# Fetching 33 of 1,568 gathered chunks row by row from SyncE and ScalarE in a two-layer graph kernel

## The chip, the cores and the metric

The kernel runs on one core of one Trainium2 chip. The metric is the device time in microseconds (us) of one execution. PE is TensorE (matmuls), DVE is VectorE, ACT is ScalarE, POOL is GpSimd, SP is SyncE, which here only issues DMAs.

## What is computed

A graph with 6,250 nodes of 128 features and 100,000 edges, sorted by receiver (`dst`), passes two message layers with a residual and a layer norm after each. Cut to what matters here:

```python
# layer 0
h = features @ W_lin.T
ef = shifted_softplus(basis(edge_weight) @ Wf1 + bf1) @ Wf2 + bf2
messages = h[senders] * ef                       # one row of h for each edge
agg = segment_sum(messages, receivers)
x = layernorm(x + shifted_softplus(agg @ Wm1 + bm1) @ Wm2 + bm2)
# layer 1
h = silu(emb @ mlp_w0 + b0); h = silu(h @ mlp_w1 + b1); w = h @ mlp_w2 + b2
ss, vv = xs[senders], xv[senders]                # one row of the new table for each edge
m = products of w, ss, vv and the unit vector of the edge
out = segment_sum(m, receivers) through W_out0, W_out1
x = layernorm(x + out / 16)
```

Both layers read one row of 128 floats (512 bytes) of a table for every edge, by the edge's sender. That read is the gather that the change is about.

## The kernel before

The edges are padded to 196 halves of 512 edges. A half has 4 chunks of 128 edges, and a pair is two halves. Each layer walks over the 196 halves. Everything is written out as straight code; every engine has its own program, and semaphores order them.

The table of a layer (`h_table` in layer 0, `up_table` in layer 1) lies in HBM. POOL gathers it: for each chunk it issues one indirect DMA (L479) that reads 128 rows by the numbers in `senders` and writes them into one of 4 slots of `sent`, a slot holding a half. Before the gathers of half n it waits until the half n-4 has been used (semaphore `msg`). So POOL issues 784 gathers in each layer.

In layer 0, SP loads the distances of a pair into `basis` (L556, L559) and stores a part of them back to HBM once ACT has worked on them (L566, `radial_embedding`). ACT makes the basis of a pair (L679, L682). PE multiplies it (`hidden0`, L885), DVE caps the sum (L1207), ACT takes exponential and logarithm (L689, L691), DVE finishes the softplus (L1216), PE applies the second weight (`filter0`, L833 and the bias L835), and DVE multiplies filter and gathered rows into `msg` (`msg0`, L1226). DVE makes the one-hot matrix of the receivers (L1187), PE sums the messages with it into a window (`window_sums`, L848), and DVE adds the window (L1200).

In layer 1, SP loads the embedding of a pair (L581, `emb_in`). PE and ACT run a small network on it (PE L904, ACT L735, PE L912, ACT L742, then `filter1`, PE L833). DVE builds `msg` in six steps (`msg1`, from L1242, which is the first to read the gathered rows, to L1261, which releases the slot), and PE sums two windows (L848, 16 matmuls a half). When the sums of 512 receivers are complete, PE runs an output unit between two halves (L1018).

The engines are staggered: at step h of its loop PE does `hidden` for half h, `filter` for half h-3 and `window_sums` for half h-5, and DVE does `msg` for half h-4. In layer 0, ACT does at step h the exponential and the logarithm of half h-2, and at every even step the basis of the pair that begins at h.

Between the layers POOL waits until all of `up_table` is stored.

## Time and profile before

| what | value |
|---|---|
| median of 3 timed runs | 2057.03 us (2056.96 to 2058.91) |
| the profiled execution, its own time | 2045.77 us |
| its span, first to last instruction | 2044.0 us |
| POOL busy | 1496.7 us, 73% |
| PE busy | 1784.7 us, 87% |
| DVE busy | 1409.2 us, 69% |
| ACT busy | 635.8 us, 31% |
| granted PE clock, mean | 0.872 of full speed |

The profiled execution is 11.3 us shorter than the median of the timed ones. Layer 0 fills the stretch from about 40 to 1,020 us of the span, and layer 1 that from about 1,040 to 2,035 us. Time in which an engine sits between two of its own instructions without waiting for another is called "issue" in the profile; on POOL it is the pause after each gather.

### The profile page before, as it was taken

Reading aid. Unit: us, or ns where it says so; the run is one execution under the profiler, and the core shown is the slowest. Engines: PE = TensorE matmul, PEld = TensorE weight load, DVE = VectorE, ACT = ScalarE, POOL = GpSimd, SP = SyncE. Lnnn points to the kernel's source line nnn. Section 1 sums busy time; section 2 is a strip of 40 time slices with the busy share of each in tenths; the row PEclk is TensorE's granted clock in tenths of the full one; section 3 lists DMA queues with packets and bytes.
Section 4 is the critical chain, followed back from the end, with each engine's and each line's share of the span. In section 5 each row is a group of like instructions: output and inputs, shape, how many; then the busy total and the mean of one; then the engine's idle time right before and its main releaser. Section 6 shows DMA issues by size and latency. Waiting matters only on the chain.

```text
span 2044.0 us, 30183 instructions
## 1 busy us (share of the span) xinstructions
PE 1784.7 (87%) x10130; PEld 1340.0 (66%) x10130; DVE 1409.2 (69%) x3184; ACT 635.8 (31%) x951; POOL 1496.7 (73%) x1610
## 2 busy tenths in 40 slices
PE   4877777877888778787869999999999999999997
PEld 4655665655666556565637777777766777777776
DVE  4785555656566666666647687687777777777876
ACT  4554443444444444444241111121121111112211
POOL 5777777777777777777647777777777777777774
PEclk8878778888788898889869898899899899889989
DMA  7322222222222232222311222222222222222232
GB/s 207 100 81 80 83 77 83 81 79 80 80 80 80 80 84 80 81 79 81 108 46 53 56 58 57 57 57 57 57 58 57 57 57 57 57 57 57 57 102 53
DMA packets 99487, 150.69 MB, mean 74 GB/s; under 512 B 33916, under 2 KB 59174, under 8 KB 99230
## 3 DMA queue, kind: packets, MB, share of 16 engines
q0 software_dynamic: 50656, 103.11, 18.7%
q1 hardware_dynamic: 48336, 43.56, 7.0%
q10 hardware_dynamic: 336, 2.01, 0.3%
q8 instruction: 87, 1.43, 0.3%
q14 instruction: 72, 0.59, 0.1%
HBM read 135.33 MB, written 13.21 MB: 73 GB/s over the span
## 4 chain that ended last, share of the span: by engine, by line
POOL 44%; PE 33%; issue 15%; DVE 2%; DMA 2%; ACT 1%; SPq 1%; DVEq 0%; POOLq 0%; ACTq 0%
POOL sent L479 44%; PE bank L848 15%; PE bank L833 7%; PE bank L912 3%; PE bank L904 3%; PE bank L835 2%; PE bank L1018 1%; PE bank L932 1%; DMA sent<-up_table,senders 1%; DMA radial_embedding<-basis 0%; ACT unit_in L650 0%; DMA x_sb<-in_x 0%; ACT unit_in L648 0%; DMA basis<-near_lengths 0%; PE bank L795 0%
## 5 line engine op out<-in xcount | busy, mean ns | idle before, releaser
L479 POOL DMA_INDIRECT sent<-up_table,senders x784 | 739.8, 944 | 267.7 <-issue 234.4
L479 POOL DMA_INDIRECT sent<-h_table,senders x784 | 739.9, 944 | 258.7 <-issue 237.8
L848 PE MATMUL bank<-onehot,msg 128*128 128x128 f32 x4704 | 732.7, 314 | 4.2 <-DVE msg L1261 3.2
L848 PEld LDWEIGHTS bank<-onehot,msg 128*128 128x128 f32 x4704 | 651.1, 219 | 116.2 <-issue 104.0
L833 PE MATMUL bank<-Wf_sb,hid 128*128 128x128 f32 x1568 | 258.6, 316 | 179.7 <-DVE msg L1226 178.0
L833 PEld LDWEIGHTS bank<-Wf_sb,hid 128*128 128x128 f32 x1568 | 227.1, 223 | 205.2 <-DVE msg L1226 201.8
L1226 DVE TENSOR_TENSOR msg<-bank,sent 128x512 f32<-128x512 f32 x196 | 135.4, 691 | 310.7 <-issue 251.2
L833 PEld LDWEIGHTS bank<-w_sb,h 64*128 64x128 f32 x1568 | 191.4, 189 | 170.6 <-issue 127.3
L1187 DVE TENSOR_TENSOR onehot<-relT,bank 128x512 f32<-128x512 f32 x392 | 265.9, 678 | 8.8 <-PE bank L848 6.2
L689 ACT ACTIVATE soft<-soft 128x512 f32<-128x512 f32 x196 | 122.9, 627 | 444.5 <-DVE soft L1207 444.4
L1200 DVE TENSOR_TENSOR sums<-sums,bank 128x128 f32 (+1 forms) x392 | 136.6, 348 | 165.7 <-PE bank L848 161.4
L833 PE MATMUL bank<-w_sb,h 64*128 64x128 f32 x1568 | 229.2, 287 | 11.0 <-DVE msg L1261 10.8
L742 ACT ACTIVATE h<-bank,cols 128x512 f32<-128x512 f32 x98 | 67.3, 687 | 426.2 <-PE bank L912 426.2
L735 ACT ACTIVATE h<-bank,cols 128x512 f32<-128x512 f32 x98 | 67.3, 687 | 370.3 <-PE bank L904 370.3
L835 PE MATMUL bank<-bias,ones_bf 3*128 3x512 bf16 x405 | 166.3, 411 | 0.0
L1242 DVE TENSOR_TENSOR dots<-sent,bank 128x384 f32<-128x384 f32 x196 | 108.5, 554 | 76.7 <-DMA sent<-up_table,senders 71.8
L885 PE MATMUL bank<-basis,Wf_sb 50*128 50x256 f32 x784 | 146.9, 507 | 13.9 <-ACT basis L682 13.9
L1207 DVE TENSOR_SCALAR soft<-bank,cols 128x512 f32<-128x512 f32 x196 | 145.0, 740 | 13.7 <-PE bank L885 8.6
L1216 DVE SCALAR_TENSOR_TENSOR hid<-bank,cols,soft 128x512 f32<-128x512 f32 x196 | 145.8, 744 | 9.8 <-ACT soft L691 9.8
L691 ACT ACTIVATE soft<-soft,half_const 128x512 f32<-128x512 f32 x196 | 141.4, 721 | 6.4
L885 PEld LDWEIGHTS bank<-basis,Wf_sb 50*128 50x128 f32 x784 | 86.0, 236 | 63.3 <-issue 39.1
L912 PE MATMUL bank<-h,w_sb 128*128 128x512 f32 x196 | 117.6, 685 | 9.4 <-ACT h L735 9.4
(140 smaller groups left out, 1399.9 us busy)
## 6 DMA issues: line engine op xcount, KB each, us to landing
basis<-in_edge_weight SPq DMA_DIRECT2D x196, 100.0 KB
sent<-h_table,senders POOLq DMA_INDIRECT x784
sent<-up_table,senders POOLq DMA_INDIRECT x784
basis<-near_lengths SPq DMA_DIRECT2D x196, 16.0 KB
radial_embedding<-basis SPq DMA_DIRECT2D x196, 16.0 KB
emb_in<-radial_embedding SPq DMA_DIRECT2D x98, 32.0 KB
x_sb<-in_x SPq DMA_DIRECT2D x12, 256.0 KB, 7.2
h_table<-h SPq DMA_DIRECT2D x12, 256.0 KB, 4.2
```

The costliest lines, as they stand in the source:

```text
L479: pool.indirect_dma_start(sent[:, n % SLOTS, j, :], None, table, bass.IndirectOffsetOnAxis(pick, 0))\
L691: a.activation(tile_, tile_, ACT.Ln, scale=0.5, bias=half_const[:, :])\
L833: t_.matmul(out_bank[0:rows, j, :], lhs(j), weight, start=(j == 0), stop=False, skip_group_check=True)
L835: return t_.matmul(out_bank[0:rows, 0:n_tiles, :], ones_bf[:, 0:rows], bias3[:, which:which + 1, :].broadcast_to([3, n_tiles, P]), start=F ...
L848: last = t_.matmul(ps[:, k, :], msg[:, p, j, k * P:(k + 1) * P], onehot[:, p, j, :], start=(j == 0), stop=(j == HALF_CHUNKS - 1))
L885: last = t_.matmul(filtA[q.slot][:, cs], Wf1_sb[rows, :], basis[rows, q.pair_slot, cs], start=True, stop=True, skip_group_check=True)
L912: t_.matmul(bank[1][:, :], w1_sb[:], h1[:, g, :], start=True, stop=True)\
L1187: v.tensor_tensor(onehot[:, p], by_chunk(relT, h).rearrange("p (j a) -> p j a", a=1) .broadcast_to([P, HALF_CHUNKS, WINDOW]), numbers[p].r ...
L1200: v.tensor_tensor(here, here, ps[:, 0:outputs, :], ALU.add).then_inc(sm["added"], 1)
L1207: v.tensor_scalar(soft[:, p, :], filtA[h.slot][:, :], bf1_c, EXP_CAP, ALU.add, ALU.min)\
L1216: v.scalar_tensor_tensor(out=hid[:, p, :], in0=filtA[h.slot][:, :], scalar=bf1_s, in1=soft[:, p, :], op0=ALU.add, op1=ALU.max)\
L1226: v.tensor_tensor(msg[:, p, :, 0:P], filtB[0], sent[:, h.slot], ALU.mult)\
```

## The change

33 chunks, 13 in layer 0 and 20 in layer 1, are no longer gathered by POOL. SP and ACT fetch them instead, one DMA of 512 bytes for each row, 128 rows a chunk, into a buffer of their own (`by_rows_sp`, `by_rows_act`, two chunks deep). ACT then copies the finished chunk into its place in `sent`. The table `row_halves` says which engine takes which chunk of a half, from which half on, how many halves lie between two such chunks, and how many rows are fetched in one pair of halves:

| layer | engine | halves between chunks | rows in a pair | chunks |
|---|---|---|---|---|
| 0 | SP | 22 | 12 | 8 |
| 0 | ACT | 32 | 8 | 5 |
| 1 | SP | 16 | 16 | 11 |
| 1 | ACT | 20 | 13 | 9 |

The row numbers are read from `src_i` in SBUF into registers, at most 7 at a time (TENSOR_LOAD); each row then takes one register instruction (ISA) and one DMA. SP does this after its own DMAs of a pair, ACT after the work of each half, half of the pair's rows at a time. DVE waits for 48 instead of 64 on `landed` for a half with one such chunk, and for the copy (`s_placed`). To make room for new semaphores, two units of `x` share one load semaphore `d_x`. A few things change in the branch for unsorted receivers too, which this input does not take.

```diff
+class Rows:
+    def __init__(self, layer, engine, chunk, start, apart, rows, halves):
...
+        self.first = start + apart + 2
+        self.count = (halves - 2 - self.first) // apart + 1
...
+    row_halves = [Rows(0, "sp", 3, 8, 22, 12, halves),
+                  Rows(0, "act", 2, 8, 32, 8, halves),
+                  Rows(1, "sp", 3, 8, 16, 16, halves),
+                  Rows(1, "act", 2, 8, 20, 13, halves)]
...
+    by_rows = {e: sb(f"by_rows_{e}", [P, 2, P]) for e in sorted({r.engine for r in row_halves})}
...
-    d_x, d_bases, d_up = sems("d_x", len(units)), sem("d_bases"), sem("d_up")
+    d_x, d_bases, d_up = sems("d_x", -(-len(units) // 2)), sem("d_bases"), sem("d_up")
...
+    def fetch_rows(eng, engine_type, r, table, some, k):
+        if len(some) == 0:
+            return
+        if some[0] == 0:
+            wait(eng, s_placed[r], k - 1)
+        pair, column = r.place(k)
+        for first in range(some[0], some[-1] + 1, 7):
+            now = range(first, min(first + 7, some[-1] + 1))
+            _, numbers_now = nc.values_load_multi_w_load_instructions(
+                src_i[pair:pair + 1, column + now[0]:column + now[-1] + 1],
...
+            for i, number in zip(now, numbers_now):
+                eng.dma_start(by_rows[r.engine][i:i + 1, k % 2, :], table[bass.ds(number, 1), :])\
+                    .then_inc(d_by_rows[r][k % 2], 16)
...
-        def gather(sm, table):
+        def gather(sm, table, layer):
...
                 for j in range(HALF_CHUNKS):
+                    if j in chunks_by_rows(layer, n):
+                        continue
...
         def move_basis(h):
...
+            if h.real():
+                own_rows(0, h.rel, h_dram)
...
         for n in range(SLOTS, halves):
             load_embedding(Half(n, halves))
+            if n % 2 == 0:
+                own_rows(1, n, v_dram)
...
+        def place_rows(layer, sm, n):
+            for r in rows_of_layer(layer):
...
+                wait(act, d_by_rows[r][k % 2], (k // 2 + 1) * P * 16)
+                wait(act, sm["msg"], n - SLOTS + 1)
+                a.activation(sent[:, n % SLOTS, r.chunk, :], by_rows[r.engine][:, k % 2, :],
+                             ACT.Copy).then_inc(s_placed[r], 1)
...
         def layer0(h):
+            place_rows(0, L0, h.rel - 2)
...
+            own_rows(0, h, h_dram)
...
         def layer1(h):
+            place_rows(1, L1, h.rel - 2)
...
+            own_rows(1, h, v_dram)
...
-            wait(dve, L0["landed"][h.slot], h.uses(64))
+            rows_there(0, L0, h)
...
-            pe.wait_ge(d_x[u.rel], 16)
+            pe.wait_ge(d_x[u.rel // 2], 16 * min(2, len(units) - u.rel // 2 * 2))
```

Where this moves instructions: on POOL, in half 32 of layer 0, the first with a chunk of SP's, the gathers of four halves stood as follows before (one that carries the wait for the slot, and three more).

```order
L479 DMA sent<-h_table,senders 128x128 [waits L0_msg]
L479 DMA sent<-h_table,senders 128x128 x3
L479 DMA sent<-h_table,senders 128x128 [waits L0_msg]
L479 DMA sent<-h_table,senders 128x128 x3
L479 DMA sent<-h_table,senders 128x128 [waits L0_msg]
L479 DMA sent<-h_table,senders 128x128 x3
```

In the changed kernel the same place has three gathers in one half.

```order
L546 DMA sent<-h_table,senders 128x128 [waits L0_msg]
L546 DMA sent<-h_table,senders 128x128 x3
L546 DMA sent<-h_table,senders 128x128 [waits L0_msg]
L546 DMA sent<-h_table,senders 128x128 x2
L546 DMA sent<-h_table,senders 128x128 [waits L0_msg]
L546 DMA sent<-h_table,senders 128x128 x3
```

One gather is gone, and nothing stands in its place on POOL.

On SP in layer 1, the loads of the embedding followed one another with only the wait for PE's first matmul (`L1_filt1`) between them.

```order
L581 DMA emb_in<-radial_embedding 16x512 [waits d_emb1,d_emb0]
L581 DMA emb_in<-radial_embedding 16x512
L589 DMA up_table<-sums 128x4x128 [waits s_rows] x12
L589 DMA up_table<-sums 106x128 [waits s_rows]
L581 DMA emb_in<-radial_embedding 16x512 [waits L1_filt1] x96
```

In the changed kernel (L664 is that load) 16 rows stand behind each one while chunks are fetched: three loads of row numbers (7, 7 and 2) and 16 times a register instruction with a DMA. The end of one such block, the next load of the embedding, and the beginning of the next block:

```order
L448 TENSOR_LOAD src_i
L452 ISA
L452 DMA by_rows_sp<-up_table 1x128
L452 ISA
L452 DMA by_rows_sp<-up_table 1x128
L664 DMA emb_in<-radial_embedding 16x512 [waits L1_filt1]
L448 TENSOR_LOAD src_i
L452 ISA
L452 DMA by_rows_sp<-up_table 1x128
```

The next load of the embedding now comes after 35 instructions that were not there.

On ACT in layer 0, logarithm (L691), basis (L679, L682) and the next exponential (L689) followed each other.

```order
L689 ACTIVATE soft<-soft 128x512 [waits L0_capped]
L691 ACTIVATE soft<-soft,half_const 128x512 [waits L0_exped]
L679 ACTIVATE basis<-basis,neg_centers 122x512 [waits L0_r_in1]
L682 ACTIVATE basis<-basis,exp_bias,exp_scale 122x512 [waits L0_squared]
L689 ACTIVATE soft<-soft 128x512 [waits L0_capped]
L691 ACTIVATE soft<-soft,half_const 128x512 [waits L0_exped]
```

In the changed kernel (L774 and L776 are the exponential and logarithm, L764 and L767 the basis) four rows stand between a logarithm and what follows it.

```order
L776 ACTIVATE soft<-soft,half_const 128x512 [waits L0_exped]
L448 TENSOR_LOAD src_i
L452 ISA
L452 DMA by_rows_act<-h_table 1x128
L452 ISA
L452 DMA by_rows_act<-h_table 1x128
L452 ISA
L452 DMA by_rows_act<-h_table 1x128
L452 ISA
L452 DMA by_rows_act<-h_table 1x128
L764 ACTIVATE basis<-basis,neg_centers 122x512 [waits L0_r_in1]
```

So the basis, or the next exponential, can begin only when these nine instructions have been issued.

## Rows read from the trace of the kernel before

**Rows 1.** POOL's waits: engine line <- waited for: us in total, times, longest

```profile
POOL sent L479 <- issue: 472.2, 1549, 0.3
POOL sent L479 <- DVE msg L1261: 9.4, 14, 4.5
```

**Rows 2.** Timeline of POOL: start, us, engine, line; first and last gather of each layer

```profile
38.46 1.04 POOL L479 DMA_INDIRECT sent<-h_table,senders  x1 [19.84 <-DMA h_table<-h]
...
1016.29 0.94 POOL L479 DMA_INDIRECT sent<-h_table,senders  x1 [0.30 <-issue]
...
1041.12 0.94 POOL L479 DMA_INDIRECT sent<-up_table,senders  x1 [23.89 <-DMA up_table<-sums]
...
2023.75 0.94 POOL L479 DMA_INDIRECT sent<-up_table,senders  x1 [0.30 <-issue]
```

**Rows 3.** Page, costliest groups: line, operation, count, busy and mean ns, idle before

```profile
L1226 DVE TENSOR_TENSOR msg<-bank,sent 128x512 f32<-128x512 f32 x196 | 135.4, 691 | 310.7 <-issue 251.2
```

**Rows 4.** Windows of layer 1: busy us of each engine, PE clock, DMA share, GB/s

```profile
1090.00:1350.00 260.00, 260.00 (x1457) 194.08 (x1456) 195.17 (x486) 37.10 (x54) 196.60 (x209) 0.89 0.21 57
1350.00:1590.00 240.00, 230.66 (x1360) 170.28 (x1360) 179.18 (x470) 42.87 (x61) 181.48 (x193) 0.95 0.21 57
1590.00:1950.00 360.00, 360.00 (x2058) 268.03 (x2056) 274.94 (x722) 67.88 (x96) 272.00 (x289) 0.91 0.21 57
```

**Rows 5.** The same windows for line L1261 alone, one instruction a half

```profile
1090.00:1350.00 260.00, 15.24 (x54) 0.89 0.21 57
1350.00:1590.00 240.00, 13.53 (x48) 0.95 0.21 57
1590.00:1950.00 360.00, 20.38 (x72) 0.91 0.21 57
```

**Rows 6.** Timeline of PE in layer 1: window sums of two halves one pair apart

```profile
1150.80 3.52 PE L848 MATMUL bank<-onehot,msg 128*128 128x128 f32 x16
...
1161.12 3.58 PE L848 MATMUL bank<-onehot,msg 128*128 128x128 f32 x16
...
1220.69 2.05 PE L848 MATMUL bank<-onehot,msg 128*128 128x128 f32 x16
...
1229.37 0.82 PE L848 MATMUL bank<-onehot,msg 128*128 128x128 f32 x5
```

**Rows 7.** Chain that ended last, layer 1: start, us, what; one output unit

```profile
1635.68 1.91 PE bank L1018 x16
```

**Rows 8.** Timeline of SP and ACT in layer 0, and ACT's DMA at 45 us

```profile
45.11 0.81 ACT L682 ACTIVATE basis<-basis,exp_bias,exp_scale 122x512 f32<-122x512 f32 x1
45.12 0.32 ACTq L702 DMA_DIRECT2D sums<-in_edge_attr  x1
...
503.32 0.30 SPq L559 DMA_DIRECT2D basis<-near_lengths  x1
503.67 0.29 SPq L556 DMA_DIRECT2D basis<-in_edge_weight  x1
```

**Rows 9.** Timeline around the start of layer 1, PE, ACT and DVE

```profile
1039.55 2.06 PE L904 MATMUL bank<-emb_in,w_sb 16*128 16x512 f32 x2 [2.76 <-issue]
...
1047.92 0.25 ACT L669 ACTIVATE inverse_all<-inverse_all 128x52 f32<-128x52 f32 x1
...
1049.53 0.69 DVE L1187 TENSOR_TENSOR onehot<-relT,bank 128x512 f32<-128x512 f32 x1 [1.81 <-issue]
```

**Rows 10.** Timeline of ACT in layer 0, one pair, and the DVE step behind

```profile
503.09 0.72 ACT L691 ACTIVATE soft<-soft,half_const 128x512 f32<-128x512 f32 x1
...
506.92 0.63 ACT L689 ACTIVATE soft<-soft 128x512 f32<-128x512 f32 x1 [1.65 <-DVE soft L1207]
507.58 0.72 ACT L691 ACTIVATE soft<-soft,half_const 128x512 f32<-128x512 f32 x1
...
510.36 0.74 DVE L1216 SCALAR_TENSOR_TENSOR hid<-bank,cols,soft 128x512 f32<-128x512 f32 x1
```

**Rows 11.** Timeline of PE, first units of the table of layer 0

```profile
7.44 1.94 PE L787 MATMUL bank<-ident,x_sb 128*128 128x128 f32 x8 [1.74 <-DMA x_sb<-in_x]
```

More of the change, by code:

```diff
@@ L16 @@
 from contextlib import ExitStack
+import itertools
 import math
@@ L192, in each_unit, with number, iterations, place @@
     for_units(eng, nodes, own, 0)
+class Rows:
+    def __init__(self, layer, engine, chunk, start, apart, rows, halves):
+        self.layer, self.engine, self.chunk = layer, engine, chunk
+        self.start, self.apart, self.rows = start, apart, rows
+        self.first = start + apart + 2
+        self.count = (halves - 2 - self.first) // apart + 1
+        assert apart % 2 == 0 and apart // 2 * rows >= P
+    def number(self, n):
+        k, rest = divmod(n - self.first, self.apart)
+        return k if rest == 0 and 0 <= k < self.count else None
+    def iterations(self):
+        return [(self.first + k * self.apart) // SLOTS for k in range(self.count)]
+    def place(self, k):
+        n = self.first + k * self.apart
+        return n // 2, n % 2 * HALF + self.chunk * P
+    def of_pair(self, n):
+        k, rest = divmod(n - self.start, self.apart)
+        if not 0 <= k < self.count:
+            return None, range(0)
+        return k, range(min(rest // 2 * self.rows, P), min((rest // 2 + 1) * self.rows, P))
 def complete_after(edges, nodes, halves):
@@ L378, in build @@
     L0, L1 = edge_sems(0), edge_sems(1)
+    d_by_rows = {r: sems(f"d_by_rows_{r.engine}{r.layer}_", 2) for r in row_halves}
+    s_placed = {r: sem(f"s_placed_{r.engine}{r.layer}") for r in row_halves}
     every = [{k: sems(f"every{n}_{k}", 2) for k in ("onehot", "window", "added")} for n in range(2)]
@@ L524, in _, with own_rows @@
         wt_halves = edge_weight.rearrange("(n e) -> n e", e=HALF)
+        def own_rows(layer, n, table):
+            for r in rows_of_layer(layer):
+                if r.engine == "sp":
+                    k, some = r.of_pair(n)
+                    if n == r.start:
+                        sp.wait_ge(d_rows[0], 16)
+                        if layer == 0:
+                            for s in range(WIDE):
+                                sp.wait_ge(table0["stored"][s], stores_of(s))
+                        else:
+                            sp.wait_ge(s_table, 16 * len(units))
+                    fetch_rows(sp, mybir.EngineType.SP, r, table, some, k)
         def load_layer1_weights():
@@ L692, in soft_log, with own_rows @@
                 .then_inc(sm[n[1]], 1)
+        def place_rows(layer, sm, n):
+            for r in rows_of_layer(layer):
+                k = r.number(n)
+                if k is None:
+                    continue
+                wait(act, d_by_rows[r][k % 2], (k // 2 + 1) * P * 16)
+                wait(act, sm["msg"], n - SLOTS + 1)
+                a.activation(sent[:, n % SLOTS, r.chunk, :], by_rows[r.engine][:, k % 2, :],
+                             ACT.Copy).then_inc(s_placed[r], 1)
+        def own_rows(layer, h, table):
+            for r in rows_of_layer(layer):
+                if r.engine == "act" and h.real():
+                    k, rows = r.of_pair(h.rel - h.parity)
+                    if h.rel == r.start:
+                        act.wait_ge(d_rows[0], 16)
+                        if layer == 0:
+                            for s in range(WIDE):
+                                act.wait_ge(table0["stored"][s], stores_of(s))
+                        else:
+                            act.wait_ge(s_table, 16 * len(units))
+                    half = len(rows) // 2
+                    fetch_rows(act, mybir.EngineType.Activation, r, table,
+                               rows[half:] if h.parity else rows[:half], k)
         def layer0(h):
+            place_rows(0, L0, h.rel - 2)
             if h.parity == 0 and h.real():
@@ L1218, in soft0, with rows_there @@
                 .then_inc(L0["soft"], 1)
+        def rows_there(layer, sm, h):
+            last = h.counter.start * SLOTS + h.rel
+            fewer = sum(len(chunks_by_rows(layer, n)) for n in range(h.slot, last + 1, SLOTS))
+            wait(dve, sm["landed"][h.slot],
+                 h.counter.value(64, (h.rel // SLOTS + 1) * 64 - 16 * fewer))
+            for r in rows_of_layer(layer):
+                if h.counter.eng is None and r.number(h.rel) is not None:
+                    wait(dve, s_placed[r], r.number(h.rel) + 1)
         def msg0(h):
@@ L1240, in msg1 @@
             wait(dve, L1["ways"], h.upto())
-            wait(dve, L1["landed"][h.slot], h.uses(64))
+            rows_there(1, L1, h)
             v.tensor_tensor(dots[:, p], vec, dirs, ALU.mult).then_inc(L1["dots"], 1)
```

25 lines of the change are left out of this document (16 added, 9 removed).

## The prediction

> **What bounds the kernel now.** I read POOL's waits first [rows 1]. Of 1,568 gathers, 1,549 wait for nothing but their own pause of 0.3 us, and only 14 of layer 1 wait for DVE, 9.4 us in all. So POOL issues gathers without a break. Its timeline gives the price of one [rows 2]: in layer 0 (1016.29 - 38.46) / 783 = 1.249 us, in layer 1 (2023.75 - 1041.12) / 783 = 1.255 us, or 1.243 us without those 9.4 us. A half costs POOL 4.99 us.
>
> An engine that never rests need not be what the others wait for, so I read the consumers next, a layer at a time. In layer 0, DVE stands idle before `msg` L1226 for 310.7 us [rows 3], 1.59 us in each of 196 halves. The consumers could take a half in 4.99 - 1.59 = 3.40 us: layer 0 is POOL's.
>
> Layer 1 is different. In the windows 1090 to 1350 and 1590 to 1950, PE is busy for all of the time [rows 4], and the count of L1261 says how many halves passed [rows 5]: 54 in 260 us (4.81 us a half) and 72 in 360 us (5.00 us). In the window between, PE was busy for 230.66 of 240 us, for 48 halves at 5.00 us. PE has two paces. From one L848 to that of a pair later it takes 10.32 us where part of the pair runs at the low clock and 8.68 us (4.34 a half) at full clock [rows 6]. The low clock (half speed, 1.2 of 2.4 GHz) takes 2 x (1 - 0.89) = 0.22, 0.10 and 0.18 of the three windows [rows 4]. A slow pair has about a third of its time there (3.4 us), and loses 1.64 us: 0.48 us lost for each low us. An output unit adds about 1.9 us [rows 7]. Check on the first window: 54 x 4.34 + 0.22 x 260 x 0.48 = 262 us, where 260 passed. So there PE alone sets the pace, and POOL's steady issue hides it, because the slots of `sent` let POOL stay ahead. A faster POOL gains only where PE waits: in the middle window PE's own work is 48 x 4.34 + 0.10 x 240 x 0.48 + 3 units x 1.9 = 225.5 us of 240. Some 14 us of waiting is all that layer 1 has to give while its clock stays as it is.
>
> **The change, part by part.**
>
> Gathers removed from POOL, layer 0: 13 x 1.249 = 16.2 us. The consumers catch up by 1.59 us in each half, and a missing gather comes at most about once in 9 halves, so all 16.2 us should arrive. Term: -16.2 us.
>
> Gathers removed in layer 1: 20 x 1.243 = 24.9 us on POOL. What arrives is PE's to decide. Upper bound within the present clock: the 14 us above. Lower bound: if the middle window becomes like its neighbours, its low share rises to the 0.20 between 0.22 and 0.18, and it takes (48 x 4.34 + 5.7) / (1 - 0.20 x 0.48) = 237 us, a gain of 3 us. The outer windows give nothing in either case. I take the middle, 9 us, since no row says which share follows when PE never waits. Term: -9 us.
>
> Row DMAs on SP. No row shows a DMA with an address from a register. The nearest is SP's static one, 0.30 us long, with 0.35 us from one start to the next [rows 8]; I take 0.34. The load of row numbers is not shown by itself either. DVE, between ACT's L669 (done at 1048.17) and its own L1187 (1049.53), does a load of one value, a branch and a load of two values, together 1.36 us [rows 9]: at most 0.68 us a load. PE shows 2.76 us [rows 9] for leaving one branch, a load and entering the next: the upper bound, and nothing is the lower. I take 0.68, the row with loads of the same kind and less else in it. The register step before each DMA has no row. DVE has one before each L1200 without a gap that I could assign to it, so I take nothing and test it below.
>
> SP in layer 1, a pair: 0.3 for the embedding + 16 x 0.34 + 3 x 0.68 = 7.8 us. By the bounds for the load it is 5.7 or 14.0 us. POOL's new pace is 2 x (4.99 - 20 x 1.25 / 196) = 9.7 us a pair. It fits with 1.9 us to spare. SP in layer 0, a pair: 6 x 0.34 + 12 x 0.34 + 2 x 0.68 = 7.5 us of 9.8. The next `basis` load waits behind these rows, but it is due two pairs before its use. Cost: nothing, covered by SP's idle time; without that cover SP sets the pace (rival 1).
>
> Row DMAs on ACT. An ACT DMA of 0.32 us was issued while an ACTIVATE of 0.81 us ran [rows 8], so ACT's issue lies beside its work. In layer 0, 4 rows after a logarithm take 4 x 0.33 + 0.68 = 2.0 us from 503.1 on. The basis then starts at about 505.1 instead of 503.7 [rows 10], and it takes some 1.5 us, until 506.7. The next exponential began at 506.92 after 1.65 us of idle time [rows 10]: just covered. Behind it, DVE's L1216 reads the logarithm at 510.36, and that logarithm ended at 508.30, so 2.06 us more are there before DVE and then PE's `filter0` come late. In layer 1, 13 rows a pair take 13 x 0.33 + 2 x 0.68 = 5.7 us of at least 8.68. Cost: nothing. If that cover failed, each us of lateness would add up to a us to a half.
>
> The copies into `sent`: 33 ACT instructions, shorter than the 0.72 us of a logarithm of four times the size; ACT does each two steps before DVE needs it. If a copy waited, the exponentials behind it and then DVE would too, but its rows are issued four halves ahead. The added waits on DVE come due earlier than `landed`. Nothing.
>
> The shared `d_x`: PE took units 0 and 1 in one run of 8 transposes at 7.44 us [rows 11], so both were there. Later pairs may wait for one load more, and POOL starts only once the last table store has landed. Between 0 and 1 us; I take 0.
>
> Sum: -16.2 - 9 = -25 us. The profiled execution, 2045.77 us, would become 2021 us. The timed runs stand 11.3 us above it, and nothing here says that this remainder changes, so the forecast for their median is 2057.03 - 25 = 2032 us.
>
> The Trainium skill bears on the price of the row numbers. Its page "Runtime: NRT & Kernel Launch", section "Instruction fetch mechanics", gives a load about 200 ns for each register. The estimate by that page is 16 x 0.2 = 3.2 us for SP's pair in layer 1 in place of 2.0, which makes the pair 8.9 us, and then a register step of 0.05 us would already use up the room. The page speaks of loads from HBM; these come from SBUF, and no run here shows it.
>
> **The rivals.**
>
> 1. SP becomes the bound in layer 1. Call R all that a row costs: its DMA, its register step and its share of a load. SP's pair is 0.3 + 16 R, by my values R = 0.47 and the pair 7.8 us. At R = 0.585 it reaches the 9.7 us of POOL's pace. SP fetches over 11 x 8 = 88 pairs. The kernel as a whole gets slower when 88 x (0.3 + 16 R - 9.99) exceeds the 16 us of layer 0: from R = 0.62 on. At R = 0.65 the pair takes 10.7 us and the kernel 88 x 0.71 - 16 = +46 us: 2103 us. For it: the register step is unpriced, and PE's 2.76 us for a load would make R 0.86. Against it: DVE's row, and the 1.9 us to spare. By the page cited above R is 0.54 before the register step, the nearest thing to this rival. Chance 0.19, and mostly far above the range.
>
> 2. PE keeps up and all 33 gathers count: 16.2 + 24.9 = 41 us, 2016 us. It needs a lower share of low clock in the windows where PE is now busy throughout; the middle window had 0.10 while PE waited a little. Against it: with POOL ahead PE waits less. Chance 0.12.
>
> 3. Layer 1 gives nothing, layer 0 everything: -16 us, 2041 us. It needs a low share of about 0.22 in the middle window. Chance 0.16.
>
> 4. The change buys nothing: layer 1 loses by a lower clock share or by late rows about what layer 0 gains, or ACT's rows delay layer 0. ACT has 2.06 us in reserve; at R = 0.65 its four rows take 2.6 us, still inside. 2057 us. Chance 0.10.
>
> **How the numbers follow.** The forecast, 2021 to 2040 us, has a chance of 0.43; with 0.12, 0.16, 0.10 and 0.19 for the rivals that is 1. A measurement tells about 0.2% (4 us) from no change. Faster by more: 0.43 + 0.12 + 0.16 = 0.71. Within: 0.10. Slower: 0.19. The range reaches from rival 2 with a little below it, 2012 us, to just above rival 4, 2062 us; it leaves out rival 1. The likeliest case's own range is 2021 to 2040 us.
>
> **What the profile after would show.** POOL should still pause 0.3 us between gathers, with the last gather of layer 0 about 16 us earlier and still few waits for L1226. In layer 1 POOL should now wait for DVE's last `msg` step for some 10 us or more, PE should be busy throughout also in its middle part, and its clock share there tells rivals 2 and 3 apart. SP's row DMAs should start 0.34 us apart, with gaps of 0.7 us at each load, and SP should still wait for PE's first matmul L904 in each pair. The forecast is wrong if those waits vanish (rival 1), if ACT's copies wait for their rows, or if DVE idles before L1216 in layer 0.

## The result and the profile after

The changed kernel takes 2115.86 us (median of 4 runs, 2113.87 to 2120.22) against 2057.97 us for the kernel before beside it (4 runs, 2056.96 to 2059.84). The ratio is 1.0286, with a 95% interval of 1.027 to 1.0301: 58 us slower. The forecast was 2032 us, and the range ended at 2062 us. What happened is rival 1, nearly at the price that it was worked out for (R = 0.65, 2103 us). Among the runs of the kernel before that stood beside the experiments below, one (2217.77 us, at a granted clock of 0.695) was in the chip's slower state and is left out.

Line numbers moved: the gather is L546 (was L479), `window_sums` L964 (L848), `msg0` L1352 (L1226), the last step of `msg1` L1387 (L1261), hidden of layer 1 L1020 (L904), the embedding load L664 (L581). The row numbers are loaded at L448 and the row DMAs issued at L452.

From the page of the changed kernel, the chain that ended last, by engine and by line, and two of the costliest groups:

```profile
span 2118.3 us, 43693 instructions
...
SPq 66%; issue 18%; PE 7%; POOL 4%; DVE 2%; DMA 1%; ACT 1%; DVEq 0%; ACTq 0%
SPq L452 32%; SPq L448 24%; POOL sent L546 4%; PE bank L964 3%; SPq L640 3%; SPq L647 2%; SPq L637 2%; PE bank L949 1%; SPq L664 1%; PE bank L1020 1%; PE bank L1028 1%; DMA x_sb<-in_x 1%; DMA radial_embedding<-basis 0%; ACT unit_in L735 0%; PE bank L951 0%
...
L1352 DVE TENSOR_TENSOR msg<-bank,sent 128x512 f32<-128x512 f32 x196 | 134.7, 687 | 81.8 <-PE bank L951 67.0
```

SP, which only issues DMAs, carries 66% of the chain, by the row DMAs (32%) and the loads of row numbers (24%). The idle time of DVE before `msg` of layer 0, which was 310.7 us because the gathers were late [rows 3], is now 81.8 us, and PE ends most of it: in layer 0 something upstream of DVE has become slow.

The waits on POOL, SP, PE, ACT and DVE (engine line <- waited for: us in total, times, longest):

```profile
POOL sent L546 <- DVE msg L1387: 115.8, 71, 5.7
...
SPq L664 <- PE bank L1020: 56.3, 8, 12.6
...
SPq L114 <- PE bank L1001: 17.8, 5, 7.4
...
PE bank L1020 <- DMA emb_in<-radial_embedding: 39.8, 32, 2.6
...
ACT basis L764 <- DMA basis<-near_lengths: 338.7, 91, 13.1
...
DVE hid L1332 <- ACT soft L776: 194.6, 82, 6.0
```

POOL now waits 115.8 us for DVE in layer 1, where it was 9.4 us [rows 1]. SP waits for PE hardly at all. The same two waits of SP before the change, not shown above, were these (L581 and L113 are now L664 and L114):

```profile
SPq L581 <- PE bank L904: 914.0, 96, 13.1
SPq L113 <- PE bank L885: 625.1, 93, 10.8
```

So 1,539 us of SP's waiting shrank to 74 us. What SP delivers is waited for instead: in layer 1 PE for the embedding (no such wait shows before), in layer 0 ACT for the `basis` load (22.7 us before) and DVE behind ACT (9.8 us before).

The first and last gathers give the two layers. These are the groups of all gathers of a layer in the changed kernel (duration in ns: least, median, most; first and last start in us):

```profile
L546 POOL DMA_INDIRECT sent<-up_table,senders x764: 939/945/962, 1037.5 to 2090.5; - x191
L546 POOL DMA_INDIRECT sent<-h_table,senders x771: 940/945/1115, 39.2 to 1009.2; - x193
```

From first to last gather layer 0 takes 970.0 us (977.8 before, by [rows 2]) and layer 1 takes 1053.0 us (982.6 before): -8 and +70 us. The stretches come from one execution of each kernel. That of the kernel before (2045.77 us) was 11 us under its median and that of the changed kernel 4 us over its own, so differences of a few us between stretches say little.

SP's timeline in the middle of layer 1 of the changed kernel shows the pair itself (start, length, line):

```profile
1507.21 0.32 SPq L664 DMA_DIRECT2D emb_in<-radial_embedding  x1
1508.89 9.06 SPq L452 DMA_DIRECT2D by_rows_sp<-up_table  x16
1518.00 0.32 SPq L664 DMA_DIRECT2D emb_in<-radial_embedding  x1
```

A pair takes 10.79 us, with no wait in it. The forecast had 7.8 us, and the kernel before took 982.6 x 8 / 783 = 10.04 us. The pair shown is one of the shorter ones. The first load of the embedding with 16 rows behind it and the first without stand here:

```profile
1057.70 0.30 SPq L664 DMA_DIRECT2D emb_in<-radial_embedding  x1
...
2022.32 24.53 SPq L664 DMA_DIRECT2D emb_in<-radial_embedding  x5
```

So the 88 pairs took (2022.32 - 1057.70) / 88 = 10.96 us each, and 88 x (10.96 - 10.04) = 81 us more than before. The other 10 pairs, without rows, took 88 us where 10 x 10.04 = 100 us stood before, and +70 us is what is left. PE's granted clock in 1045 to 2000 us fell too, from 0.90 to 0.86. It did not set this pace, since SP waited for nothing inside the pairs. The chain through that pair says what a row is made of (start, length, what):

```profile
1507.57 1.15 SPq L448
...
1510.57 0.23 SPq L452
1510.80 0.05 issue
1510.85 0.04 SPq L452
1510.89 0.04 issue
1510.92 0.03 SPq L452
1510.95 0.03 issue
1510.98 0.23 SPq L452
...
1511.66 1.77 SPq L448
```

From one row DMA to the next it is 10.98 - 10.57 = 0.41 us: 0.23 for the DMA and 0.18 for two short register instructions and the gaps around them. A load of seven numbers took 1.15 us once and 1.77 us the next time. All loads together (ns: least, median, most):

```profile
L448 SPq TENSOR_LOAD <-src_i x440: 538/1224/1900, 77.3 to 2020.7; - x147
L448 ACTq TENSOR_LOAD <-src_i x340: 479/952/1948, 80.6 to 2042.1; - x170
```

So R = (10.79 - 0.32) / 16 = 0.654 us in the pair shown, and 0.665 us by the mean pair.

The three loads of a pair kept their order of size through all 88 pairs: 1.15 us for rows 0 to 6, 1.79 us for rows 7 to 13, 0.75 us for the last two (means). What tells the two loads of seven apart is where their numbers stand. I sorted all 1,402 loads of SP in four traces (the changed kernel, **edge**, **lighter**, **best**) by how many numbers they read, and by whether the first of these stands at a multiple of four in its chunk (a chunk's 128 numbers begin at a multiple of 128 in a row of `src_i`). Median us, with the number of loads:

| numbers in the load | first at a multiple of four | first elsewhere |
|---|---|---|
| 1 | 0.55 (20) | 0.54 (165) |
| 2 | | 0.74 (88) |
| 3 | | 0.95 (84) |
| 4 | 0.57 (18) | |
| 5 | | 1.37 (80) |
| 6 | 1.01 (36) | 1.57 (126) |
| 7 | 1.19 (409) | 1.74 (376) |

The two groups of seven don't overlap (1.09 to 1.48 us and 1.63 to 1.96 us). Elsewhere each number adds about 0.20 us; from a multiple of four on, the first four numbers together cost what one does.

### The profile page after: what moved, and what is told of

The parts are those of the page before. It is cut to its first block, busy times and chain, and to the rows that moved or that the text cites. A ratio compares the mean times of both kernels' runs of the same rounds, so it can differ in the third digit from the quotient of the medians.

```text
span 2118.3 us, 43693 instructions
## 1 busy us (share of the span) xinstructions
PE 1803.4 (85%) x10130; PEld 1368.2 (65%) x10130; DVE 1419.6 (67%) x3184; ACT 643.9 (30%) x984; POOL 1467.6 (69%) x1577
## 4 chain that ended last, share of the span: by engine, by line
SPq 66%; issue 18%; PE 7%; POOL 4%; DVE 2%; DMA 1%; ACT 1%; DVEq 0%; ACTq 0%
SPq L452 32%; SPq L448 24%; POOL sent L546 4%; PE bank L964 3%; SPq L640 3%; SPq L647 2%; SPq L637 2%; PE bank L949 1%; SPq L664 1%; PE bank L1020 1%; PE bank L1028 1%; DMA x_sb<-in_x 1%; DMA radial_embedding<-basis 0%; ACT unit_in L735 0%; PE bank L951 0%
## 5 line engine op out<-in xcount | busy, mean ns | idle before, releaser
L546 POOL DMA_INDIRECT sent<-up_table,senders x764 | 721.9, 945 | 359.5 <-issue 216.3
L546 POOL DMA_INDIRECT sent<-h_table,senders x771 | 729.0, 946 | 262.8 <-issue 232.8
L964 PE MATMUL bank<-onehot,msg 128*128 128x128 f32 x4704 | 763.5, 323 | 7.3 <-DVE sums L1316 4.4
L964 PEld LDWEIGHTS bank<-onehot,msg 128*128 128x128 f32 x4704 | 679.3, 227 | 124.0 <-issue 113.1
L1001 PE MATMUL bank<-basis,Wf_sb 50*128 50x256 f32 x784 | 140.5, 487 | 198.7 <-ACT basis L767 198.7
L949 PEld LDWEIGHTS bank<-w_sb,h 64*128 64x128 f32 x1568 | 200.5, 197 | 165.9 <-issue 157.4
L1332 DVE SCALAR_TENSOR_TENSOR hid<-bank,cols,soft 128x512 f32<-128x512 f32 x196 | 146.6, 748 | 200.3 <-ACT soft L776 194.6
L949 PE MATMUL bank<-Wf_sb,hid 128*128 128x128 f32 x1568 | 248.0, 310 | 13.0 <-DVE msg L1352 12.1
L949 PE MATMUL bank<-w_sb,h 64*128 64x128 f32 x1568 | 239.9, 296 | 0.6 <-DVE msg L1387 0.5
L1352 DVE TENSOR_TENSOR msg<-bank,sent 128x512 f32<-128x512 f32 x196 | 134.7, 687 | 81.8 <-PE bank L951 67.0
L764 ACT ACTIVATE basis<-basis,neg_centers 122x512 f32<-122x512 f32 x98 | 70.6, 721 | 340.8 <-DMA basis<-near_lengths 338.7
L774 ACT ACTIVATE soft<-soft 128x512 f32<-128x512 f32 x196 | 121.6, 621 | 155.3 <-issue 114.0
L1020 PE MATMUL bank<-emb_in,w_sb 16*128 16x512 f32 x196 | 116.1, 673 | 42.2 <-DMA emb_in<-radial_embedding 39.8
L776 ACT ACTIVATE soft<-soft,half_const 128x512 f32<-128x512 f32 x196 | 141.4, 722 | 6.4
```

The costliest lines, as they stand in the source:

```text
L546: pool.indirect_dma_start(sent[:, n % SLOTS, j, :], None, table, bass.IndirectOffsetOnAxis(pick, 0))\
L776: a.activation(tile_, tile_, ACT.Ln, scale=0.5, bias=half_const[:, :])\
L949: t_.matmul(out_bank[0:rows, j, :], lhs(j), weight, start=(j == 0), stop=False, skip_group_check=True)
L964: last = t_.matmul(ps[:, k, :], msg[:, p, j, k * P:(k + 1) * P], onehot[:, p, j, :], start=(j == 0), stop=(j == HALF_CHUNKS - 1))
L1001: last = t_.matmul(filtA[q.slot][:, cs], Wf1_sb[rows, :], basis[rows, q.pair_slot, cs], start=True, stop=True, skip_group_check=True)
L1020: t_.matmul(bank[0][:, :], w0_sb[:], emb_in[:, g, :], start=True, stop=True)\
```

## The experiments

Each was compared with the kernel before on its own chip. The stretches from first to last gather are from the profiled execution of each. The kernel before took 2056.47 us beside **gone**, **static**, **only0** and **only1**, 2057.57 us beside **fixed_loads**, **sp_only**, **act_only** and **lighter**, and 2058.09 us beside **first_of_seven**, **edge** and **best** (medians of 13, 13 and 16 runs). Its runs spread over some 17 us there (2048 to 2065 us in the first), so a single median says less than its ratio's interval. The ratio is estimated from the single runs and is not the quotient of two medians. The executions that the stretches come from lay up to 10 us from their kernel's own median (**act_only** 9 us over, **edge** on it, **best** 10 us under).

| kernel | median us | ratio (95%) | layer 0, us | layer 1, us |
|---|---|---|---|---|
| before | 2057 | | 977.8 | 982.6 |
| changed | 2115.86 | 1.0286 (1.027 to 1.0301) | 970.0 | 1053.0 |
| gone | 2018.64 | 0.9839 (0.9787 to 0.9892) | 965.1 | 962.7 |
| static | 2029.74 | 0.9865 (0.9808 to 0.9922) | 964.0 | 973.0 |
| fixed_loads | 2021.71 | 0.9835 (0.9784 to 0.9885) | 963.9 | 962.0 |
| only0 | 2046.19 | 0.9946 (0.9925 to 0.9968) | 968.3 | 985.0 |
| only1 | 2129.51 | 1.0352 (1.0306 to 1.0397) | 980.1 | 1057.5 |
| sp_only | 2122.79 | 1.0319 (1.0274 to 1.0365) | 976.1 | 1051.4 |
| act_only | 2046.33 | 0.9945 (0.9919 to 0.9972) | 973.4 | 985.9 |
| lighter | 2033.79 | 0.9899 (0.9841 to 0.9957) | 965.8 | 967.2 |
| first_of_seven | 2027.24 | 0.9884 (0.9833 to 0.9935) | 965.1 | 965.2 |
| edge | 2053.5 | 0.9983 (0.9967 to 0.9999) | 978.2 | 983.9 |
| best | 2029.06 | 0.9886 (0.9848 to 0.9923) | 965.2 | 960.6 |

**gone: the gathers left out, and nobody fetches.** The 33 chunks keep what was in their slot. This measures what POOL's relief is worth by itself.

```diff
     def rows_of_layer(layer):
-        return [r for r in row_halves if r.layer == layer]
+        return []
     def chunks_by_rows(layer, n):
-        return [r.chunk for r in rows_of_layer(layer) if r.number(n) is not None]
+        return [r.chunk for r in row_halves if r.layer == layer and r.number(n) is not None]
```

> Leaves out the 33 gathers and fetches their rows nowhere (no row DMAs, no loads of row numbers, no copies; those chunks use what the slot held before), so only POOL's relief is left. If SP's issue of rows is the cause of the loss, this is faster than before by the 16 us of layer 0 and 3 to 14 us of layer 1: about 2033 us, 2025 to 2040. If it is PE that cannot follow in layer 1 at all, 2042 us. If the loss comes from something else that a faster POOL sets off (a lower clock of PE), it stays above 2058 us.

Measured: 2018.64 us, ratio 0.9839, 33 us by the ratio and 12.7 + 19.9 = 33 us by the two stretches. So the relief exists, and 33 of the 41 us that POOL saves arrive, 8 more than the forecast's sum. The windows of layer 1 of this kernel (us, PE busy, PEld, DVE, ACT, POOL, clock, DMA share, GB/s) stand against [rows 4]:

```profile
1090.00:1350.00 260.00, 260.00 (x1459) 193.91 (x1458) 195.34 (x491) 36.84 (x54) 196.07 (x208) 0.89 0.22 57
1350.00:1590.00 240.00, 240.00 (x1377) 177.96 (x1377) 183.94 (x472) 42.87 (x61) 181.26 (x193) 0.91 0.22 57
1590.00:1950.00 360.00, 360.00 (x2119) 267.20 (x2119) 282.24 (x745) 71.22 (x102) 268.88 (x285) 0.94 0.22 56
```

PE is busy throughout, as forecast; in the middle part the clock fell from 0.95 to 0.91, but in the last part it rose from 0.91 to 0.94, which the forecast held to give nothing. PE has two clock levels, 1.2 and 2.4 GHz, and 0.94 says that 0.12 of the time was at the lower. The share there is not fixed, and the forecast had treated it as if it were.

**static: the 33 chunks fetched at fixed rows.** No loads of numbers and no register step; all row DMAs and copies remain. The rows fetched are other rows than the senders'.

```diff
-            _, numbers_now = nc.values_load_multi_w_load_instructions(
-                src_i[pair:pair + 1, column + now[0]:column + now[-1] + 1],
...
+            numbers_now = [(pair * PAIR + column + i * 37) % nodes for i in now]
...
-                eng.dma_start(by_rows[r.engine][i:i + 1, k % 2, :], table[bass.ds(number, 1), :])\
+                eng.dma_start(by_rows[r.engine][i:i + 1, k % 2, :], table[number:number + 1, :])\
```

> All 33 chunks are fetched by 128 DMAs each from SP and ACT, but from fixed rows, written into the program: no load of row numbers and no register step (so the wrong rows are used). If instruction time on SP is the cause, its pair in layer 1 shrinks from 10.8 to 0.3 + 16 x 0.34 = 5.8 us, below POOL's 9.7 us, and the time is that of the kernel without the 33 gathers, about 2033 us. If the 4,224 small transfers themselves cost (DMA engines, landing times, ACT's copies), it stays near 2116 us.

Measured: 2029.74 us, ratio 0.9865. SP in layer 1:

```profile
1506.77 4.78 SPq L450 DMA_DIRECT2D by_rows_sp<-up_table  x16
...
1516.73 0.31 SPq L662 DMA_DIRECT2D emb_in<-radial_embedding  x1
```

Sixteen rows take 4.78 us, 0.30 us each, and then SP waits for PE for 5.2 us. 4,224 transfers of 512 bytes, their semaphores and the 33 copies cost nothing that can be told from **gone** (0.9808 to 0.9922 against 0.9787 to 0.9892). The loss lies in turning numbers in SBUF into addresses. SP's pairs here last 8.68 or 10.3 us for the most part, the two paces that PE has at full clock and with a stretch of the low one [rows 6].

**fixed_loads: meant to be static with its loads kept.** The program that was built dropped them, since nothing used the numbers: no TENSOR_LOAD is in its trace.

```diff
+            numbers_now = [(pair * PAIR + column + i * 37) % nodes for i in now]
...
-                eng.dma_start(by_rows[r.engine][i:i + 1, k % 2, :], table[bass.ds(number, 1), :])\
+                eng.dma_start(by_rows[r.engine][i:i + 1, k % 2, :], table[number:number + 1, :])\
```

> As the fixed rows (no register step, the wrong rows are used), but the loads of row numbers stay in place, unused. The trace of the change shows SP's loads at 1.2 us in the middle of their spread for 7 numbers and 0.7 for 2. By these SP's pair in layer 1 is 0.3 + 16 x 0.30 + about 3.9 = 9.0 to 9.7 us, at or just below POOL's 9.7: 2030 to 2045 us, with SP nearly without waits for PE. If the loads alone are the cause, it stays near 2100 us; if only the register step and the DMAs count, it is the 2030 us of the fixed rows.

Measured: 2021.71 us, ratio 0.9835. It says nothing of the loads, so whether they alone would make the loss wasn't measured, and it is a repeat of **static**. As one it is useful: the same program's layer 1 took 973.0 and 962.0 us in the two profiled executions, so 11 us of layer 1 come and go by themselves.

**only0 and only1: one layer at a time.**

```diff
 (only0)
                   Rows(0, "act", 2, 8, 32, 8, halves),
-                  Rows(1, "sp", 3, 8, 16, 16, halves),
-                  Rows(1, "act", 2, 8, 20, 13, halves)]
 (only1)
-    row_halves = [Rows(0, "sp", 3, 8, 22, 12, halves),
-                  Rows(0, "act", 2, 8, 32, 8, halves),
```

> The 13 chunks of layer 0 alone; layer 1 as before. By SP's issue as the bound: SP needs 9.95 us for a pair in layer 0, POOL without 13 gathers 9.8 us, so the last gather of layer 0 comes 7 us earlier, as in the trace of all 33: about 2051 us. By the prediction's prices it would be 16 us, 2042 us. If ACT's rows were the loss, 2058 us or more.

> The 20 chunks of layer 1 alone; layer 0 as before. By SP's issue as the bound: 88 pairs at 10.8 us where they took 9.99, +70 us between the first and the last gather as in the trace of all 33: about 2123 us. If the loss came from layer 0's changed SP stream or from both together, it would be below 2100 us.

Measured: 2046.19 us (0.9946) and 2129.51 us (1.0352). The loss is layer 1's. Layer 0 gained 9.5 us where **gone** gains 12.7 there.

**sp_only and act_only: one engine at a time.** SP's 19 chunks without ACT's 14, and the reverse.

```diff
 (sp_only)
-                  Rows(0, "act", 2, 8, 32, 8, halves),
...
-                  Rows(1, "act", 2, 8, 20, 13, halves)]
 (act_only)
-    row_halves = [Rows(0, "sp", 3, 8, 22, 12, halves),
...
-                  Rows(1, "sp", 3, 8, 16, 16, halves),
```

> SP's 19 chunks alone, ACT fetches none. By SP's issue as the bound nothing gets better, since SP's program is the same: about 2116 us, with the last gather of layer 1 some 1050 us after the first. If ACT's rows were a part of the loss (exponentials, h1 and h2 late), it is below 2095 us.

> ACT's 14 chunks alone. ACT's rows take 13 x 0.41 + 2 x 1.1 = 7.5 us of a pair in layer 1 and 2.6 us of a half in layer 0, both inside its idle time: 14 x 1.25 = 17.5 us faster on POOL, about 2040 us. If ACT's rows are a bound of their own, 2056 us or more.

Measured: 2122.79 us (1.0319) and 2046.33 us (0.9945). SP's share alone makes all of the loss, in layer 1 by the same stretch as the whole change (1051.4 against 1053.0 us), and its 88 pairs take the same 10.96 us each. In layer 0 SP's 8 chunks brought 1.7 us of 10. ACT's share makes no loss: its 5 chunks of layer 0 brought 4.4 of 6.2 us. In layer 1 its 9 chunks brought nothing in the profiled execution, which was the slowest of ten (2055.48 us).

**lighter: SP's rows thinned until its pair fits.** 28 chunks in place of 33.

```diff
-    row_halves = [Rows(0, "sp", 3, 8, 22, 12, halves),
+    row_halves = [Rows(0, "sp", 3, 8, 32, 8, halves),
...
-                  Rows(1, "sp", 3, 8, 16, 16, halves),
+                  Rows(1, "sp", 3, 8, 20, 13, halves),
```

> All four streams, SP with as few rows a pair as ACT: 8 in layer 0 (every 32 halves), 13 in layer 1 (every 20 halves); 28 chunks in all. SP's pair is 0.3 + 13 x 0.41 + 2 x 1.4 = 8.4 us in layer 1 and 2.0 + 8 x 0.41 + 1.2 + 0.5 = 7.0 us in layer 0, below POOL's 9.7 and 9.8. By SP's issue as the bound this turns the loss into a gain of 28/33 of the 38 us that the kernel without the 33 gathers showed: about 2025 us, 2018 to 2040. If a loss comes with any use of SP for rows, above 2058 us.

Measured: 2033.79 us, ratio 0.9899. Three rows fewer in a pair of layer 1 (and four fewer in layer 0) turn +58 us into -21 us by the ratio. The number of rows fetched doesn't explain it: **sp_only** fetches 19 chunks and loses, this one fetches 28 and gains. SP waits for PE again:

```profile
SPq L664 <- PE bank L1020: 147.2, 60, 11.7
```

**first_of_seven: the loads kept, part of the register step taken out.** All rows of a load use its first number, so six of seven rows are the wrong ones.

```diff
-            for i, number in zip(now, numbers_now):
+            for i, number in zip(now, numbers_now[:1] * len(now)):
```

> The change, but the rows of a load all use its first number: a load of 7 numbers stands as before in front of 7 rows, and one register instruction (ISA) follows it in place of 7. The rows fetched are the wrong ones for 6 of 7. In the changed kernel SP's pair of layer 1 took 0.35 + 16 x 0.41 + 3.7 (three loads) = 10.7 us. Theory A (the sum of all parts of a row makes SP the bound, and none alone does): the rows stand 0.30 us apart, SP's pair is 0.35 + 4.8 + 3.7 = 8.9 us, under the 9.7 us at which POOL can go, and the time is that of the kernel with fixed rows, 2020 to 2040. Rival B (the loads alone suffice, because each holds SP until the transfers before it have been handed on, so that they grow when the rows stand closer): the pair stays at 10 us or more and the time above 2060.

Measured: 2027.24 us, ratio 0.9884, and a pair of SP in layer 1:

```profile
1504.32 0.32 SPq L664 DMA_DIRECT2D emb_in<-radial_embedding  x1
1505.99 7.95 SPq L452 DMA_DIRECT2D by_rows_sp<-up_table  x16
1513.99 0.32 SPq L664 DMA_DIRECT2D emb_in<-radial_embedding  x1
```

The pair took 9.67 us and not the 8.9 us expected. One short register instruction (MOVE) was left before each DMA, so the rows stand 0.33 us apart and not 0.30; the three loads and their gaps take the rest, 9.67 - 0.35 - 16 x 0.33 = 4.0 us. Even so the time is that of the theory that SP's whole pair decides: 1.1 us less in a pair, from 10.8 to 9.7 us (from 10.96 to 9.82 us by the mean of 88), and the loss of 2.9% is a gain of 1.2%. In 1090 to 1990 us SP waited for PE in only 6 pairs, so this kernel stands exactly where SP and the other engines take turns. The rival, that the loads grow when the rows stand closer, is not borne out: the three loads took 3.69 us a pair in both kernels.

**edge: SP alone, 15 rows in a pair and every 18th half.** 10 chunks, a test just at the threshold.

```diff
-    row_halves = [Rows(0, "sp", 3, 8, 22, 12, halves),
-                  Rows(0, "act", 2, 8, 32, 8, halves),
-                  Rows(1, "sp", 3, 8, 16, 16, halves),
-                  Rows(1, "act", 2, 8, 20, 13, halves)]
+    row_halves = [Rows(1, "sp", 3, 8, 18, 15, halves)]
```

> Only SP, only layer 1, 15 rows in a pair and every 18th half (10 chunks in place of 33). SP's pair is then 0.35 + 15 x 0.41 + 3.6 = 10.1 us, where the halves went by at 9.99 us a pair before. Theory A (the time of layer 1 follows SP's pair as soon as it is the longest): 94 pairs at 10.1 in place of 9.99 us, +5 to +15 us: 2060 to 2075, and SP waits no longer for PE. Rival B (something else than SP's pair, such as rows that come late for ACT's copy, costs the time): 10 chunks less for POOL bring 2040 to 2050.

Measured: 2053.5 us, ratio 0.9983 (0.9967 to 0.9999), in the gap between the two ranges expected, 6.5 us below theory A's and 3.5 us above the rival's. So the test as it was set decides for neither. Its timeline says why:

```profile
1583.86 0.32 SPq L661 DMA_DIRECT2D emb_in<-radial_embedding  x1
1586.45 8.50 SPq L449 DMA_DIRECT2D by_rows_sp<-up_table  x15
1595.00 0.32 SPq L661 DMA_DIRECT2D emb_in<-radial_embedding  x1
1597.25 7.95 SPq L449 DMA_DIRECT2D by_rows_sp<-up_table  x15
1605.25 0.32 SPq L661 DMA_DIRECT2D emb_in<-radial_embedding  x1
1606.93 3.77 SPq L449 DMA_DIRECT2D by_rows_sp<-up_table  x8
1610.76 0.32 SPq L661 DMA_DIRECT2D emb_in<-radial_embedding  x1
```

The pairs with 15 rows shown take 11.1 and 10.3 us (10.65 by the mean of all 80), but every ninth has the remaining 8 rows and takes 5.5 us. I had left that out of the expectation. The mean of the 90 pairs is then 10.08 us, against 10.04 us before. Layer 1 went by in 983.9 us, as before the change (982.6), although POOL had 12.5 us less to do, and SP's waits for PE fell from 914.0 us to 44.6 us. That is what SP at its old pace would give, but this reading was made after the result.

With 15 rows a pair, a load of seven begins now at a multiple of four and now not. These are the first loads of the second and the third pair shown, which begin at rows 105 and 120 of the chunk (ns: least, median, most of the one load):

```profile
L445 SPq TENSOR_LOAD <-src_i x1: 1730/1730/1730, 1595.4 to 1595.4; - x1
L445 SPq TENSOR_LOAD <-src_i x1: 1162/1162/1162, 1605.6 to 1605.6; - x1
```

Both stand right behind the embedding's DMA, so what stands before a load is not what makes it dear.

**best: what the arithmetic proposes.** SP at 10 and 13 rows, ACT as in the change, 29 chunks.

```diff
-    row_halves = [Rows(0, "sp", 3, 8, 22, 12, halves),
+    row_halves = [Rows(0, "sp", 3, 8, 26, 10, halves),
...
-                  Rows(1, "sp", 3, 8, 16, 16, halves),
+                  Rows(1, "sp", 3, 8, 20, 13, halves),
```

> SP with 10 rows a pair (every 26th half) in layer 0 and 13 (every 20th) in layer 1, ACT as in the change: 29 chunks in place of 33. SP's pair: layer 0 0.6 + 10 x 0.41 + 2.4 + its own DMAs, about 8.8 us; layer 1 0.35 + 13 x 0.41 + 3.2 = 8.9 us, below 9.7. Theory A: 29 chunks x 1.25 = 36 us less on POOL, of which most arrives: 2020 to 2035, and SP waits for PE again in most pairs of both layers. If the time follows the number of rows and not SP's pair: above 2080.

Measured: 2029.06 us (6 runs, 2018.63 to 2046.38), ratio 0.9886 (0.9848 to 0.9923): 23 us faster than the kernel before, and 87 us faster than the change. Its two waits of SP:

```profile
SPq L664 <- PE bank L1020: 137.8, 61, 12.2
SPq L647 <- ACT basis L767: 60.0, 30, 8.5
```

SP has room again, with four chunks fewer than the change. It isn't told apart from **lighter** (0.9899).

## Why the prediction was wrong

**The step that failed: "Row DMAs on SP".** It took 0.34 us for a row's DMA, 0.68 us for a load and nothing for the register step, so R = 0.47 and a pair of 7.8 us. The trace gives 0.41 us from row to row and 1.15, 1.77 and 0.74 us for the three loads, so R = 0.654 and 10.79 us in the pair shown; the mean of 88 pairs is 10.96 us. Of the 3.0 us that are missing, the rows make 16 x 0.07 = 1.1 us and the loads, with the gaps around them, the remaining 1.9 us. By these parts neither alone would have done it: the limit was R = 0.585. With the rows as measured and the loads as assumed a pair takes 0.35 + 6.56 + 2.04 = 8.95 us; with the loads as measured and rows of 0.34 us it takes 0.35 + 5.44 + 3.9 = 9.7 us, just at POOL's pace. **first_of_seven** showed this second case: 9.67 us and a gain. The first case was not run.

The way to the wrong number was the choice of the row. The term had a lower end at nothing and an upper end at PE's 2.76 us, and 0.68 us was taken since DVE's two loads and a branch fitted into 1.36 us [rows 9]. Those are loads of one and two values. On SP these take 0.54 and 0.74 us, so the row was a fair witness for its size; it was none for loads of seven, at 1.19 or 1.74 us. Which of these two a load costs depends on where its numbers stand, which nothing in the change looked after. An estimate from the table: four loads of four numbers, each from a multiple of four on, take 4 x 0.57 = 2.3 us in place of 3.69, and 16 rows a pair would come to some 9.6 us, at or just under POOL's 9.7. This was not run. And "nothing" for the register step was taken because no gap could be assigned, which is not the same as having seen that there is none. The bounds themselves (5.7 to 14.0 us) were right and held both the limit of 9.7 us and the truth; the chance of 0.19 was too small for a threshold that lay inside them.

The Trainium skill, page "Runtime: NRT & Kernel Launch", section "Instruction fetch mechanics", gives a load 200 ns for each register, 3.2 us for the pair; the three loads took 1.15 + 1.77 + 0.74 = 3.66 us, 0.23 us a number. So the trace roughly agrees: away from multiples of four each further number added 0.20 us, on top of some 0.34 us for the load itself. The page speaks of loads from HBM, and these read SBUF. An estimate by the page's figure gives 8.9 us for the pair before the register step and 0.3 + 16 x 0.41 + 3.2 = 10.1 us with the measured one, above the limit.

**Rival 1 was priced rightly once R was known.** At R = 0.65 it gave a pair of 10.7 us, +62 us in layer 1 and 2103 us. Measured were 10.96 us by the mean pair, +70 us and 2115.86 us. The mean pair alone would have added 88 x 0.26 = 23 us to its +62 us. But it set the pair against 9.99 us, layer 0's pace, where layer 1's was 10.04 us (4 us), and left out that the 10 pairs without rows catch up 12 us. Layer 0 gave 8 us and not 16.

**Layer 0: -16.2 us expected, -8 us measured.** SP's price was off here too. The forecast had 7.5 us for a pair; in the changed kernel it runs without a wait:

```profile
505.98 0.29 SPq L637 DMA_DIRECT2D basis<-in_edge_weight  x1
...
509.57 6.27 SPq L452 DMA_DIRECT2D by_rows_sp<-h_table  x12
515.93 0.29 SPq L637 DMA_DIRECT2D basis<-in_edge_weight  x1
```

That is 9.95 us. But each chunk's eleventh pair has only 8 rows left, and by the mean of all 88 pairs SP takes 9.82 us, which is POOL's new pace (2 x (4.99 - 13 x 1.25 / 196) = 9.8 us). So SP had no room left in layer 0, yet POOL lost little by it. What POOL lost are waits for DVE's `msg` in the first 150 us, here in the kernel before, in **gone** and in the changed kernel:

```profile
POOL sent L479 <- DVE msg L1226: 1.1, 3, 0.5
...
POOL sent L546 <- DVE msg L1352: 4.6, 3, 3.9
...
POOL sent L546 <- DVE msg L1352: 9.1, 7, 4.3
```

In **gone** they grew by 3.5 us, nearly all of it one wait at 67 us, and 16.2 - 3.5 = 12.7 us is what arrived. In the changed kernel they grew by 8.0 us, by that wait and one at 147 us, and 16.2 - 8.0 = 8.2 us is near the 7.8 us that arrived. The forecast let all 16.2 us arrive, since the consumers are faster on average; it had no term for the start of the layer.

**Layer 1's gain: -9 us expected, -20 us there to be had.** The forecast allowed 3 to 14 us, because it held PE's share of low clock to be given. With the gathers gone the stretch shrank by 19.9 us, near rival 2's 24.9. The mechanism was right (PE busy in all windows, POOL waiting: 16.6 us in **gone**), the term was mis-sized. How much comes varies: two executions of one program gave 9.6 and 20.6 us. What sets the clock's share from execution to execution stays open.

**What held.** POOL's price of a gather held. ACT's rows and copies cost nothing that can be told: **act_only** is faster than before by 11 us, and with all of them in it **first_of_seven** has the same two stretches as **gone** within 3 us. 4,224 small transfers and their semaphores cost nothing that can be told (**static**). And the sum, had SP fitted: -25 us forecast, 23 us measured with **best**, 21 with **lighter**, 28 and 34 with **static** and its repeat. The forecast named the sign of its own failure too, that SP's waits for L904 vanish, and they did: 914.0 us before, 56.3 us after. Another sign that it named came too, DVE idling before the softplus of layer 0 (L1216, now L1332): 9.8 us before, 194.6 us after. It had meant this for ACT's rows, but **act_only** shows 10.8 us and **sp_only** 94.6 us: SP's late `basis` begins it, and ACT's rows on top make it longer. No wait of ACT's copies for their rows shows in the trace.

## What to carry to other kernels

An engine that waits half its time is not free by that: before work is moved onto it, add up all that one loop pass asks of it, and compare that sum with the pace at which the others *will* run. Here the room was 1.9 us by the forecast and below zero in truth, and beyond the limit every 0.1 us counted 88 times, while below it no loss could be told. So where a threshold lies inside the bounds of an unpriced instruction, the sensible change is the one that stays under it at the upper bound that is still likely (in **best**, 4 chunks fewer gave up 5 us on POOL and made the kernel 87 us faster than the change).

When a price is borrowed from another row, borrow it per unit: a load of two values does not price a load of seven. And when the same instruction has two prices, sort all of its records by what the program knows of each; here that took no further run.

## What the runs showed of the hardware

- A row's DMA issued by SP with an address from a register takes 0.23 us to issue, one with a fixed address 0.25 us (**static**). But the first needs two short register instructions, and comes to 0.41 us from start to start against 0.30 us. With one of the two register instructions left it is 0.33 us (**first_of_seven**).
- A load of numbers from SBUF into registers on SP took about 0.34 us and 0.20 us for each number, 1.74 us for seven. Where the first number stood at a multiple of four (16 bytes), the first four cost 0.57 us together, and seven took 1.19 us (1,402 loads in four traces).
- SP stood still for 0.34 us once in every 128 of its recorded instructions in the row pairs of layer 1, wherever the 128th fell. A pair has 52 of them (the embedding's DMA, 3 loads and 16 times two register instructions and a DMA), so two pairs in five are longer by it. One such pause, in the chain of the changed kernel between a register instruction and its DMA, where 0.03 us is usual:

```profile
1498.22 0.34 issue
```

- The Trainium skill, page "DMA: Bandwidth & Descriptors", section "Latency and other measured facts", states a floor of some 600 ns for such a load; the least seen in the changed kernel was 0.54 us on SP and 0.48 us on ACT, and 0.45 us on SP in **lighter**, so the trace agrees with the order, not with a floor.
- 4,224 transfers of 512 bytes beside the running gathers moved the time by nothing that can be told: the ratio was 0.9865 with them (**static**) and 0.9839 without (**gone**), each known to about 0.5%.
